# Cross-attention and low-rank FFN on one core: scores of the second half moved next to the weighing of the values, two buffers for turned z, and a new order on every engine for tiles 2 to 13

## What is computed

```python
def attention(query, kv):                    # 16 heads of 32
    q, k, v = query @ Wq + bq, kv @ Wk + bk, kv @ Wv + bv
    attn = softmax(clip(q k^T * scale, -1e4, 1e4))        # over 77 context rows
    return (attn @ v) @ Wo + bo
def ffn(x):
    return gelu((x @ U1) @ V1 + b1) @ U2 @ V2 + b2        # rank 128, width 2048
x = x + attention(layernorm(x), ctx)
x = x + ffn(layernorm(x))
```

## Time and profile before

| what | value |
|---|---|
| median of three runs | 556.4 us |
| the profiled execution, its own time | 556.49 us |
| its span in the trace | 554.7 us |
| what lies outside of the span | 1.8 us |
| granted TensorE clock | 1.0 of full speed |
| first stage up to the scores of tile 14 | 268.1 us of the span |
| one tile of the first stage, middle | 18.5 us |

### The profile page before, as it was taken

One profiled execution on the slowest core, in us unless ns is written; L12 is line 12 of the kernel. 1 busy time (PEld: TensorE's weight loads), 2 busy tenths in 40 slices (PEclk: granted clock), 3 DMA queues, 4 the chain that ended last, 5 costly groups with the idle time before them and its releaser, 6 DMA issues.

```text
span 554.7 us, 12050 instructions
## 1 busy us (share of the span) xinstructions
PE 544.9 (98%) x4818; PEld 463.3 (84%) x4818; DVE 475.0 (86%) x694; ACT 310.7 (56%) x524; POOL 371.9 (67%) x295
## 2 busy tenths in 40 slices
PE   8999999999999999999999999999999999999997
PEld 8998889888988898889877777888888888888885
DVE  5799989888988898889899568989889797978694
ACT  4655454545554555454455546757575757666563
POOL 1788776778777877786679356747484656565581
PEclk9999999999999999999999999999999999999999
DMA  8522352221223122243312130031121212101012
GB/s 306 187 84 76 123 222 94 97 94 63 94 96 112 45 95 97 84 151 129 134 69 73 71 114 1 19 104 49 64 88 59 76 72 82 58 19 58 20 57 95
DMA packets 25695, 50.36 MB, mean 91 GB/s; under 512 B 2984, under 2 KB 3368, under 8 KB 25256
## 3 DMA queue, kind: packets, MB, share of 16 engines
q1 hardware_dynamic: 25352, 49.07, 25.4%
q10 hardware_dynamic: 288, 0.52, 0.3%
HBM read 32.49 MB, written 16.78 MB: 89 GB/s over the span
## 4 chain that ended last, share of the span: by engine, by line
PE 85%; DVE 7%; POOL 3%; ACT 2%; DMA 1%; issue 1%; SPq 1%; DVEq 0%; POOLq 0%
PE bank L1059 50%; PE ps_s L1059 15%; PE bank L1137 6%; PE ps_s L1111 5%; PE bank L1153 5%; PE bank L1184 2%; PE bank L1080 2%; DMA ss<-in_wq 1%; DVE once L879 1%; DVE ssum L847 1%; POOL wqo_r L422 1%; POOL ss L433 1%; DVE wqo_r L884 1%; DVE hs_r L902 1%; POOL ss L441 1%
## 5 line engine op out<-in xcount | busy, mean ns | idle before, releaser
L524 POOL TENSOR_TENSOR hs_r<-ss,hs_r 128x512 fp32r<-128x512 f32 x63 | 88.3, 1401 | 91.3 <-ACT hs_r L755 91.3
L667 ACT ACTIVATE ss<-ps_s,once 128x512 f32<-128x512 f32 x128 | 88.1, 689 | 65.1 <-PE ps_s L1059 61.6
L1059 PE MATMUL ps_s<-p1t_r,v_r 128*128 128x512 f32 x384 | 111.0, 398 | 0.0
L1059 PE MATMUL bank<-hs_r,u_r 128*128 128x512 f32 x381 | 107.2, 390 | 0.0
L1059 PE MATMUL bank<-zt_r,wqo_r 128*128 128x256 f32 x768 | 97.7, 283 | 0.1
L433 POOL TENSOR_TENSOR ss<-ss,smax 128x1232 f32<-128x1232 f32 x32 | 74.9, 2339 | 33.2 <-DVE smax L842 33.2
L1059 PE MATMUL bank<-wqo_r,ot_r 128*128 128x512 f32 x384 | 95.5, 398 | 0.0
L1059 PEld LDWEIGHTS bank<-zt_r,wqo_r 128*128 128x128 f32 x768 | 91.7, 188 | 1.4 <-issue 0.3
L1059 PEld LDWEIGHTS bank<-hs_r,u_r 128*128 128x128 f32 x381 | 71.4, 188 | 15.7 <-DVE hs_r L902 0.2
L1059 PEld LDWEIGHTS bank<-wqo_r,ot_r 128*128 128x128 f32 x384 | 69.8, 188 | 13.4 <-DVE ot_r L855 0.2
L1059 PEld LDWEIGHTS ps_s<-p1t_r,v_r 128*128 128x128 f32 x384 | 69.8, 188 | 13.4 <-issue 0.4
(11 more groups left out here) (97 smaller groups left out, 816.3 us busy)
## 6 DMA issues: line engine op xcount, KB each, us to landing
xs<-in_x SPq DMA_DIRECT2D x64, 256.0 KB, 3.2
y_between<-xs SPq DMA_DIRECT2D x32, 256.0 KB, 2.0
fw<-y_between SPq DMA_DIRECT2D x4, 1024.0 KB, 5.3
xs<-y_between SPq DMA_DIRECT2D x4, 1024.0 KB, 5.5
out<-fw SPq DMA_DIRECT2D x16, 256.0 KB, 2.0
out<-xs SPq DMA_DIRECT2D x15, 256.0 KB, 2.0
xs<-in_Wo SPq DMA_DIRECT2D x1, 1024.0 KB, 8.8
fw<-in_v SPq DMA_DIRECT2D x1, 1024.0 KB, 5.1
```

What stands on the lines that cost most here:

```text
L524: pool.tensor_tensor(hs[:, c % 4, 1, :], hg[:, c % 4, :], hs[:, c % 4, 0, :].bitcast(F32), ALU.subtract)\
L667: act.activation(hg[:, c % 4, :], ps_s[:, c % 4, :], ACT.Gelu_apprx_tanh, bias=b1_c[:, c:c + 1]).then_inc(h_gelu, 1)
L1059: mm = pe.matmul(ps, lhs(a), rhs(c), start=first and i == 0, stop=last and i == len(PASSES) - 1)
```

## The change

Turned z had one buffer, zt_r. It gets a second one, in the space of hs_r (which only the FFN uses): even tiles keep theirs in the one, odd tiles in the other. For tiles 2 to 13 the lists of all four engines are written anew. For tiles 2 to 12 (`middle`) PE does, after project_out(n-2, 0): turn_probs part 2, turn_z(n+2, 0), q(n+1, second half), project_out(n-2, 1), turn_z(n+2, 1), all three parts of turn_probs(n-1, 1), scores(n, 1), weigh_values(n-1), and then scores(n+1, 0). Part 2 of the second half's probabilities goes to the bank B7, and so waits for y_sum(n-2, 1) (`y_done`). The maxima, exponent, sums and normalisation of the second half of n, and heads_low(n-1), come in tile n+1. Tile 13 still does its second half within the tile, and so has both that of 12 and its own on VectorE. Lists of tiles 0, 1, 14 and 15 are those of before.

The core of the diff, with removed lists left out:

```diff
-        hs = sb("hs_r", [P, 4, 2, TB], F32R)
+        hs_t = sb("hs_r", [P, 4 * 2 * TB], F32R)
+        hs = hs_t[:, :].rearrange("p (s h t) -> p s h t", s=4, h=2)
+        zt = [t[:, ASIDE:2 * KD * TA + ASIDE].rearrange("p (h k t) -> p h k t", h=2, k=KD) for t in (zt_t, hs_t)]
...
+        def middle(j, b):
+            return 2 <= 2 * j + b < NA - 3
+        def pt_bank(j, b, u, part):
+            return B7 if part == 2 and u and middle(*shift(j, b, 1)) else (B5, B6, B5)[part]
...
@@ GpSimd, body @@
+                    old = shift(j, b, -1)
+                    if is_block(2, j, b):
+                        normalise(*old, 1)
+                    else:
+                        subtract_max(*old, 1)
+                    x_plus_bo(*old, 0)
+                    x_plus_bo(*old, 1)
+                    subtract_max(j, b, 0)
+                    if not is_block(2, j, b):
+                        normalise(*old, 1)
+                    normalise(j, b, 0)
                     if 0 <= 2 * j + b - UV0 - 1 < NUV:
                         uv_low(2 * j + b - UV0 - 1)
+                    if there(NA, j, b, 3):
+                        rstd_of(*shift(j, b, 3))
+                    if not middle(j, b):
                         subtract_max(j, b, 1)
...
@@ ScalarE, body @@
+                    old, new = shift(j, b, -1), shift(j, b, 1)
+                    q_copy(*new, 0)
+                    copy_probs(*old, 0, (0, 1))
+                    if not is_block(2, j, b):
+                        exponent(*old, 1)
+                    copy_probs(*old, 0, (2,))
+                    turned_z(j + 1, b, (0,))
+                    exponent(j, b, 0)
+                    q_copy(*new, 1)
                     if 0 <= 2 * j + b - UV0 < NUV:
                         uv_high(2 * j + b - UV0)
+                    copy_probs(*old, 1, (0, 1, 2))
+                    turned_z(j + 1, b, (1,))
+                    if not middle(j, b):
+                        exponent(j, b, 1)
+                    heads_high(*old)
...
@@ VectorE, body @@
+                    old = shift(j, b, -1)
+                    if not is_block(2, j, b):
+                        maxima(*old, 1)
+                        heads_low(j - 1, b)
+                    norm_z(j + 1, b, (0,))
+                    clip(j, b, 0)
+                    maxima(j, b, 0)
+                    if not is_block(2, j, b):
+                        sums(*old, 1)
+                    y_sum(j - 1, b, 0)
+                    turned_z(j + 1, b, (0,))
+                    norm_z(j + 1, b, (1,))
+                    sums(j, b, 0)
                     for u in range(2):
                         if there(NA, j, b, 3):
                             norm_stats(*shift(j, b, 3), u)
                         else:
                             norm_stats2(0, 0, u)
+                    if middle(j, b):
+                        y_sum(j - 1, b, 1)
+                        clip(j, b, 1)
+                        turned_z(j + 1, b, (1,))
+                    else:
+                        clip(j, b, 1)
+                        maxima(j, b, 1)
+                        y_sum(j - 1, b, 1)
+                        turned_z(j + 1, b, (1,))
+                        sums(j, b, 1)
+                        heads_low(*old)
...
@@ TensorE, turn_probs and body @@
+                    elif part == 1 and there(NA, j, b, 3) and n:
+                        pe.wait_ge(zt_lo, 2 * (n + 3) + 1)
+                    elif part == 2 and bk_ is B7:
+                        pe.wait_ge(y_done, 2 * n)
...
+                    old, new = shift(j, b, -1), shift(j, b, 1)
+                    scores(j, b, 0)
+                    project_q(*new, 0)
+                    turn_probs(*old, 0, (0, 1))
...
+                    project_out(j - 1, b, 0)
+                    turn_probs(*old, 0, (2,))
                     turn_z(j + 1, b, (0,))
+                    project_q(*new, 1)
+                    if middle(j, b):
                         project_out(j - 1, b, 1)
+                        turn_z(j + 1, b, (1,))
+                        turn_probs(*old, 1, (0, 1, 2))
+                        scores(j, b, 1)
+                    else:
+                        scores(j, b, 1)
+                        turn_probs(*old, 1, (0, 1))
+                        project_out(j - 1, b, 1)
+                        turn_probs(*old, 1, (2,))
+                        turn_z(j + 1, b, (1,))
+                    weigh_values(*old)
```

More of the change, by code:

```diff
@@ L476, in rstd2_of, with first_tiles @@
                 pool.tensor_tensor(rstd_b[:, :, 0], var_b[:, :, 0], mhalf[:, :], ALU.pow).then_inc(rstd2, 1)
-            def body(j):
-                for b in range(2):
[L480 to L493, removed]
+            def first_tiles():
+                subtract_max(0, 0, 0)
+                subtract_max(0, 0, 1)
+                normalise(0, 0, 0)
+                rstd_of(1, 1)
+                shift_of(1, 1)
+                normalise(0, 0, 1)
+                subtract_max(0, 1, 0)
+                x_plus_bo(0, 0, 0)
+                x_plus_bo(0, 0, 1)
+                subtract_max(0, 1, 1)
+                normalise(0, 1, 0)
+                rstd_of(2, 0)
@@ new lines, in last_tiles @@
+            def last_tiles():
+                j = NA // 2 - 1
+                normalise(j - 1, 1, 1)
+                subtract_max(j, 0, 0)
+                rstd2_of(0, 0)
+                x_plus_bo(j - 1, 1, 0)
+                x_plus_bo(j - 1, 1, 1)
+                subtract_max(j, 0, 1)
+                normalise(j, 0, 0)
+                u1_v2_low()
+                normalise(j, 0, 1)
+                subtract_max(j, 1, 0)
+                x_plus_bo(j, 0, 0)
+                subtract_max(j, 1, 1)
+                normalise(j, 1, 0)
+                x_plus_bo(j, 0, 1)
+                normalise(j, 1, 1)
+                x_plus_bo(j, 1, 0)
+                x_plus_bo(j, 1, 1)
@@ L538, in _, with turned_z @@
         def _(act):
-            def turned_z(j, b):
+            def turned_z(j, b, us=(0, 1)):
                 n = 2 * j + b
-                for u in range(2):
+                for u in us:
                     bk_ = z_bank(j, b, u)
                     act.wait_ge(zt_full, 2 * n + u + 1)
-                    act.activation(zt[:, 0, :, u * P:(u + 1) * P],
+                    act.activation(zt[b][:, 0, :, u * P:(u + 1) * P],
                                    bk_[:, :].rearrange("p (k t) -> p k t", k=KD), ACT.Copy).then_inc(zt_hi, 1)
@@ L1119, in turn_probs @@
                 for part in parts:
-                    bk_ = (B5, B6, B5)[part]
+                    bk_ = pt_bank(j, b, u, part)
                     if part == 0:
@@ L1304, in body @@
                 for b in range(2):
[L1305 to L1320, removed]
+                    old, new = shift(j, b, -1), shift(j, b, 1)
+                    scores(j, b, 0)
+                    project_q(*new, 0)
+                    turn_probs(*old, 0, (0, 1))
+                    if is_block(2, j, b):
+                        pe.wait_ge(wo_lo, 1)
+                        pe.wait_ge(zt_lo, 8)
+                    project_out(j - 1, b, 0)
+                    turn_probs(*old, 0, (2,))
                     turn_z(j + 1, b, (0,))
-                    if there(NA, j, b, -2):
+                    project_q(*new, 1)
+                    if middle(j, b):
                         project_out(j - 1, b, 1)
-                    turn_z(j + 1, b, (1,))
-                    if before:
-                        weigh_values(*shift(j, b, -1))
+                        turn_z(j + 1, b, (1,))
[8 more added lines that the diff above has]
+                    weigh_values(*old)
             def last_tiles():
```

57 lines of the change are left out of this document (13 added, 44 removed).

## The result

The changed kernel takes 568.05 us (median of six runs, 567.54 to 569.61) against 556.75 for the kernel before on the same chips: 1.0201 times, 95% interval 1.0185 to 1.0216. It is slower, as forecast, but by 11.3 us where 4.5 were forecast, and outside the range that ended at 563.0.

The account below looks back on a forecast made before the run. PE was taken to bound the kernel now, and a ring through VectorE the middle tiles after the change. -0.15 + 2.3 + 0.15 + 2.2 = +4.5 us gave 561.0 us, range 556.8 to 563.0.

Parts of the forecast that it names:

- What PE gains: PE, each tile: dropped array-mode changes save 0.28 us, a new one costs 0.13, so 18.37 us are needed.
- Scores to values: PE's new change between tiled forms: 0.13 us taken, 0.11 of gap and 0.02 of slow first group; bounds 0 to 0.20.
- The ring: Dependency loop through VectorE, GpSimd and PE: 18.74 us per tile in tiles 3 to 12, +2.3 us in all.
- y_sum to PE: Hand-over from VectorE's y_sum to PE's transposes inside the ring, taken as 0.15 us.
- the two transposes to the scores: PE's step from two transposes to the scores behind them inside the ring, taken as 0.31 us.
- Tile 2: Claimed to have no deferred work yet and to run at PE's pace: -0.15 us.
- Tile 13: SyncE's stores of y and loads of x were costed at nothing; this tile was forecast at 18.67 us.
- The tail: VectorE's two second halves in tile 13 make its sums 2.6 us late; 2.2 us stay in the last tiles.
- its rivals: PE keeps pace, 554.8 us (0.18); only tile 13's load paid, 557.2 (0.09); longer ring, 562.7 (0.10); full 0.20 switch, forecast time.

Follow-up runs that it names:

- Experiment 1: Changed kernel with VectorE's two statistics of tiles 2 to 12 moved from ahead of y_sum to behind it: 563.47 us, 1.0133 times the kernel before.
- experiment 4: Changed kernel with the edits of Experiment 1, Experiment 2 and Experiment 3 together: 558.30 us, 1.0033 times the kernel before.
- experiment 6: Changed kernel with one more statistic on VectorE ahead of y_sum in tiles 2 to 12: 573.75 us.
- Experiment 3: Changed kernel with GpSimd's subtract_max(2, 0) put ahead of the two x_plus_bo in tile 2: 566.25 us, 1.0187 times the kernel before.
- experiment 5: Kernel before with only GpSimd's last split of the FFN weights moved behind normalise(12, 0): 558.41 us, 1.0024 times the kernel before.
- Experiment 2: Changed kernel with SyncE's two loads of the first FFN block moved behind tile 12's loads of x: 563.34 us, 1.0123 times the kernel before.
- experiment 7: The kernel of experiment 4 with tile 13's two statistics on VectorE moved behind the low part of turned z: 556.42 us, 1.0005 times the kernel before.

## Why the prediction was right or wrong

**What PE gains: right.** The 0.15 per tile came out as 0.13 (18.39 against 18.52, experiments 1 and 4). Scores to values costs 0.11 of gap, as taken, not nothing. This is also the one place where the Trainium skill (TensorEngine Tiling (Array Packing), Key Properties) spoke on the change: a new tiling mode drains the engine. The trace agrees as far as the price goes: the 0.22 from 176.99 to 177.21 are the same as from scores to transposes, so the change between two tiled forms is paid like one out of them.

**The ring: right.** 18.74 forecast, 18.73 measured, with the two long norm_z, the idle time in one piece and the wait of PE where the text had put them. Two details were off against each other: y_sum to PE took 0.06 (175.05 + 0.67 to 175.78), not 0.15, and the two transposes to the scores 0.37, not 0.31. Experiments 1 and 6 show that it is the ring: 1.5 us less in it and the tile falls to PE's 18.39, 0.6 more and the tile grows by 0.59.

**Tile 2: wrong, 3.0 us.** The step that failed is "Tile 2 still has no deferred work and runs at PE's pace". It looked at VectorE alone. GpSimd's list of tile 2 does have something new in front, the two x_plus_bo ahead of subtract_max(2, 0), 2.5 us that the ring of tile 2 can't take. Experiment 3 moves the one back and tile 2 takes 18.40. Experiment 1 leaves them there and takes 1.5 us out of the ring: 18.40 too. So it took both, the late subtract_max and the long ring.

**Tile 13: wrong, 7.5 us, the largest part.** The step that failed is "both transfers have several us before their users. I cost all of these at nothing". It went through SyncE's queue for a middle tile, and did not ask which waits SyncE has in single tiles. It also took both kinds of loads of x for ones that wait for norm_z; `load_xb`, the one for which x_plus_bo waits, waits for the stores of y. `uv_low` had been moved behind both normalises, and in tile 12 SyncE waits for the last of them ahead of stores and loads of x. The price was then raised twice: by what GpSimd's new list has behind x_plus_bo (experiment 5: the late x alone cost 1.3 us in the old order), and by the clock, which fell in PE's wait.

**The tail: right in mechanism and size, hidden in the result.** 2.2 us forecast; in the changed kernel the tail was 0.2 us longer, as VectorE caught up while everybody waited in tile 13: its sums of tile 13 start 0.49 us behind the scores of tile 14 (280.67, 280.18) where 2.6 were forecast. Experiment 2 takes that wait away and has 2.2 us.

**The clock: not in the sum.** The forecast had the waits of PE as time and no more. In three of the stretches looked at above, the clock fell behind a wait and took 1.2 to 1.7 us on top: 1.5 in tile 2 (3.43 against 1.96 for the weighing alone), 1.7 in tile 13 (26.18 less 5.85 of waiting and the 18.66 of experiment 2), 1.2 in experiment 4. The first two are part of the 3.0 and the 7.5.

The account closes: 4.5 forecast, 3.0 and 7.5 for tiles 2 and 13, less 2.0 for the covered tail, less 0.7 for small things (tile 3 was 0.2 shorter; tiles 4 to 12 grew by 0.21 each and not by 0.23, 0.2 in all; tile 2 took 18.71 before where the forecast had reckoned with 18.52; 0.1 ahead of tile 2) is 12.3. The span grew by 12.3, the medians by 11.3, as the profiled execution was 0.7 above its median and the one of before 0.3 below. Of the 12.3 only some 2 us (the ring) are a cost that the forecast had at its full price, and none of its rivals had tile 2 or tile 13.

## What to carry to other kernels

When an order is rewritten on all engines, lay the new lists beside each other for a middle turn, and then once more for the first, the last and every turn in which an engine has a step of its own; a DMA queue counts as an engine, with each wait in it and all that stands behind it. Idle time of an engine is air only if its next instruction doesn't depend, by way of others, on its own last one: close the ring and add it up before taking the idle time for a reserve.

## What the runs showed of the hardware

In tiles 4 to 12 of the changed kernel both norm_z were started while a GpSimd operation ran, and took 1.50 and 1.64 us instead of 0.54, each ending 0.28 to 0.29 us behind that operation. In tile 3 they took 0.81 and 1.23, in tile 2 the second took 1.91, and these too ended 0.28 to 0.29 behind it. The clash of the earlier trace rows repeats so exactly that it can be added up like an instruction.

PE's granted clock fell from 1.0 to 0.5 of full speed (2.4 to 1.2 GHz) after PE had idled for 5.85 us in tile 13, after 1.28 us in tile 2, and after 1.89 us in tile 15 of experiments 4 and 5. It stayed up after the same 1.28 us in tile 2 and 1.90 us in tile 15 in experiment 2, after 1.38 in experiment 7, and after 1.86 in tile 2 of experiment 6. So the length of the wait alone doesn't decide it. What does, the runs here don't settle; no kernel was made to try it.
